# A linear attention and mixture-of-experts kernel: one weight transfer per expert, seven gather buffers, and more of the down projection in split form

## The reference

```python
x = _layernorm(x + attention(x))      # decayed linear attention, 16 heads
x = _layernorm(x + moe(x))

# moe, T = 4096 rows, H = 512, E = 64 experts, K = 6, CAP = 128, I = 192
scores = softmax(xf @ gate_w.T)
topk_w, topk_idx = top_k(scores, K)
gx = xp[buf_tok]                                      # (E, CAP, H) rows of each expert
gu = einsum('ech,ehi->eci', gx, gate_up_proj)         # 512 -> 384
g, u = split(gu, 2, axis=-1)
hid = silu(g) * u                                     # 192 wide
eo = einsum('eci,eih->ech', hid, down_proj) * buf_w   # 192 -> 512
routed = zeros.at[buf_tok].add(eo)
shared = silu(xf @ shared_gate_w.T) * (xf @ shared_up_w.T) @ shared_down_w.T
```

## Time and profile before

| | us |
|---|---|
| median of 3 runs | 913.0 |
| lowest, highest | 909.56, 913.59 |
| profiled execution, its own time | 914.21 |
| span of the profiled execution | 911.6 |
| PE busy | 892.3 |
| DVE busy | 718.9 |
| ACT busy | 549.0 |
| POOL busy | 488.1 |

### The profile page before, as it was taken

One profiled execution on the slowest core, in us unless ns is written; L12 is line 12 of the kernel. 1 busy time (PEld: TensorE's weight loads), 2 busy tenths in 40 slices (PEclk: granted clock), 3 DMA queues, 4 the chain that ended last, 5 costly groups with the idle time before them and its releaser, 6 DMA issues. The chain is left out here.

```text
span 911.6 us, 15597 instructions
## 1 busy us (share of the span) xinstructions
PE 892.3 (98%) x4635; PEld 727.5 (80%) x4635; DVE 718.9 (79%) x1422; ACT 549.0 (60%) x1208; POOL 488.1 (54%) x540
## 2 busy tenths in 40 slices
PE   8999999999999999999999999999999999999997
PEld 7788888888888788777888788888788888877875
DVE  6997887979788897898857788887778887736776
ACT  5532535434353443544558878888778888736785
POOL 2002366565566656577434656766566666533665
PEclk9999999999999999999999999999999999999999
DMA  6343563536263333439567999999999999959963
GB/s 211 97 161 116 145 140 103 133 89 173 74 188 96 123 103 116 144 101 336 181 224 238 333 360 354 357 337 323 348 342 347 336 346 324 298 106 391 378 249 129
DMA packets 111634, 203.95 MB, mean 224 GB/s; under 512 B 18496, under 2 KB 50240, under 8 KB 110528
## 3 DMA queue, kind: packets, MB, share of 16 engines
q1 hardware_dynamic: 91024, 159.87, 51.2%
q0 software_dynamic: 19520, 35.75, 16.3%
q10 hardware_dynamic: 1008, 7.34, 2.1%
HBM read 143.03 MB, written 59.88 MB: 223 GB/s over the span
## 5 line engine op out<-in xcount | busy, mean ns | idle before, releaser
L1612 POOL DMA_INDIRECT slot_table<-tokens,slot_of x162 | 180.3, 1113 | 86.9 <-issue 50.4
L1657 POOL DMA_INDIRECT acc_rows<-eo,table_sb x64 | 137.1, 2142 | 119.8 <-DMA acc_rows<-eo,table_sb 61.8
L1717 PE MATMUL bank<-x_hi,wqkv_hi 128*128 128x512 f32 x384 | 152.1, 396 | 1.6 <-DVE wqkv_lo L1022 1.6
L1717 PE MATMUL bank<-x_hi,wqkv_lo 128*128 128x512 f32 x384 | 150.1, 391 | 0.0
L1717 PE MATMUL bank<-x_lo,wqkv_hi 128*128 128x512 f32 x384 | 150.1, 391 | 0.0
L1454 DVE TENSOR_TENSOR wgu_lo<-wgu,wgu_hi 128x1536 fp32r<-128x1536 f32 x64 | 112.1, 1752 | 2.6 <-ACT wgu_hi L904 1.9
L904 ACT CAST wgu_hi<-wgu 128x1536 fp32r<-128x1536 f32 x64 | 94.2, 1473 | 1.6 <-issue 0.4
L1646 POOL DMA_INDIRECT xg<-x_rows,table_sb x64 | 73.4, 1147 | 36.3 <-issue 19.0
L1717 PE MATMUL bank<-wgu_hi,xgt_hi 128*128 128x384 f32 x256 | 91.9, 359 | 0.0
L674 ACT ACTIVATE e<-bank 128x512 f32<-128x512 f32 x64 | 38.0, 594 | 81.4 <-PE bank L1717 81.4
L1717 PEld LDWEIGHTS bank<-x_hi,wqkv_hi 128*128 128x128 f32 x384 | 72.2, 188 | 17.5 <-DVE wqkv_lo L1022 1.8
(11 more groups left out here) (198 smaller groups left out, 2300.0 us busy)
## 6 DMA issues: line engine op xcount, KB each, us to landing
wgu<-w_gu SPq DMA_DIRECT2D x64, 768.0 KB, 7.3
wdn<-w_down SPq DMA_DIRECT2D x64, 384.0 KB, 8.0
xres<-x SPq DMA_DIRECT2D x32, 256.0 KB, 3.4
x_turned<-x1t SPq DMA_DIRECT2D x32, 256.0 KB, 2.9
x_rows<-x SPq DMA_DIRECT2D x32, 256.0 KB, 3.1
acc_rows<-x SPq DMA_DIRECT2D x32, 256.0 KB, 2.8
fin<-acc_rows SPq DMA_DIRECT2D x8, 1024.0 KB, 11.9
odd<-acc_rows SPq DMA_DIRECT2D x8, 1024.0 KB, 13.9
```

The costliest lines, as they stand in the source:

```text
L1612: pool.indirect_dma_start(table_dram, bass.IndirectOffsetOnAxis(slot_of[:, i, k:k + 1], 0), tokens[:, i:i + 1], None, bounds_check=SLOTS - ...
L1657: pool.indirect_dma_start(acc_dram[e % 2], bass.IndirectOffsetOnAxis(table_sb[:, e:e + 1], 0), eo[eo_slot[e]][:, :], None, bounds_check=T ...
L1717: mm = pe.matmul(out_ap, a, b, start=first and i == 0, stop=final and i == len(products) - 1)
```

## The change

Three things are changed.

**Weights.** The gate, up and down weights of an expert stand side by side in DRAM (`w_expert`, 2304 floats per partition) and are loaded by one transfer (`load_expert`, 1152 KB) into one of five joint buffers. It waits for `eo_mm` of the expert five back, as the down weights did. Before the loop, expert 1 is loaded as a whole where its down weights were loaded.

**Gathers.** There are seven buffers instead of six, `gather` runs five experts ahead instead of four, and in a pass it stands before `add_rows`.

**Plain down rows.** For 40 of the 64 experts (`split_first(e)`: a unit in pass `e` or in pass `e-1`, so 0, 1, 3, 4, 6, 7, ...) the plain down rows are split too: ACT makes one more copy (`wdn_hi`, 128x512), DVE one more subtraction (`wdn_lo`, 128x512), ACT copies the turned hidden values in one instruction of 256 columns instead of two of 128, DVE's `het_lo` has 256 columns instead of 128, and PE runs three `fp32r` products instead of one in `f32`.

```diff
-    NG, ND, NXG, AHEAD = 5, 5, 6, 4
+    NW, NXG, AHEAD = 5, 7, 5
...
+    def split_first(e):
+        return any(fills_of[max(e - 1, 0):e + 1])
...
-            def load_gate_up(e):
-                if e >= NG:
-                    sp.wait_ge(gu_mm, e - NG + 1)
-                sp.dma_start(wgu_buf[e % NG][:, :, :], w_gu[e]).then_inc(gu_in[e % NG], 16)
-
-            def load_down(e):
-                if e >= ND:
-                    sp.wait_ge(eo_mm, e - ND + 1)
-                sp.dma_start(wdn_buf[e % ND][:, :], w_down[e]).then_inc(dn_in[e % ND], 16)
+            def load_expert(e):
+                if e >= NW:
+                    sp.wait_ge(eo_mm, e - NW + 1)
+                sp.dma_start(we_buf[e % NW][:, :], w_expert[e]).then_inc(we_in[e % NW], 16)
...
             sp.wait_ge(state_done, STEPS)
-            for e in range(2, NG - 1):
-                load_gate_up(e)
-            load_down(2)
+            load_expert(2)
...
             sp.wait_ge(heads_mm, NB)
-            load_down(3)
+            load_expert(3)
             sp.wait_ge(shared_split, 2)
-            for e in range(2):
-                load_gate_up(e)
+            load_expert(0)
...
             sp.wait_ge(shared_split, 2 + SC)
-            for e in range(2):
-                load_down(e)
+            load_expert(1)
...
-            load_gate_up(NG - 1)
-            load_down(ND - 1)
-            for e in range(NE):
-                if e + NG < NE:
-                    load_gate_up(e + NG)
-                if e and e - 1 + ND < NE:
-                    load_down(e - 1 + ND)
+            for e in range(4, NE):
+                load_expert(e)
...
             def split_down_of(e):
-                act.wait_ge(dn_in[e % ND], 16 * (e // ND + 1))
+                act.wait_ge(we_in[e % NW], 16 * (e // NW + 1))
                 if e >= 2:
                     act.wait_ge(eo_mm, e - 1)
-                w, mix = wdn_buf[e % ND], wdn_mix[e % 2]
+                w, mix = wdn_buf[e % NW], wdn_mix[e % 2]
+                if split_first(e):
+                    act.copy(wdn_hi[e % 2][:, :], w[:, 0:D])
...
-                act.copy(hid_et[e % 2][:, :], ht_ps[:, 0:P])
-                act.copy(het_hi[e % 2][:, :], ht_ps[:, P:2 * P]).then_inc(het_hi_done, 1)
+                if split_first(e):
+                    act.copy(het_hi[e % 2][:, :], ht_ps[:, 0:2 * P]).then_inc(het_hi_done, 1)
+                else:
+                    act.copy(hid_et[e % 2][:, :], ht_ps[:, 0:P])
+                    act.copy(het_hi[e % 2][:, P:2 * P], ht_ps[:, P:2 * P]).then_inc(het_hi_done, 1)
...
+                if split_first(e):
+                    dve.tensor_tensor(wdn_lo[e % NW][:, :], w[:, 0:D], wdn_hi[e % 2][:, :].bitcast(F32), ALU.subtract)
...
+                cols = slice(0 if split_first(e) else P, 2 * P)
+                dve.tensor_tensor(het_lo[e % 2][:, cols], ht_ps[:, cols], het_hi[e % 2][:, cols].bitcast(F32),
...
             for e in range(NE):
+                if e + AHEAD < NE:
+                    gather(e + AHEAD)
                 if e >= 2:
                     add_rows(e - 2)
-                if e + AHEAD < NE:
-                    gather(e + AHEAD)
...
-                chain(eo_ps[:, :], [(hid_et[e % 2][:, :], wdn_buf[e % ND][:, 0:D])], first=False).then_inc(eo_mm, 1)
+                if split_first(e):
+                    products = three(het_hi[e % 2][:, 0:P], het_lo[e % 2][:, 0:P], wdn_hi[e % 2][:, :], wdn_lo[e % NW][:, :])
+                else:
+                    products = [(hid_et[e % 2][:, :], wdn_buf[e % NW][:, 0:D])]
+                chain(eo_ps[:, :], products, first=False).then_inc(eo_mm, 1)
```

More of the change, by code:

```diff
@@ L89, in build @@
                                                           for s in ("sum", "mean", "square", "rstd", "shift")]
-    wgu_at = [both.at + 4 * i * KC * GU for i in range(2)]
-    wgu_buf = [both.place(f"wgu{i}", [P, KC, GU]) for i in range(2)]
-    wdn_buf = [both.place(f"wdn{i}", [P, DN]) for i in range(2)]
+    we_at = [both.at + 4 * i * WE for i in range(2)]
+    we_buf = [both.place(f"we{i}", [P, WE]) for i in range(2)]
     att = Map(nc, both.at, end)
@@ L197, in build @@
     late = Map(nc, projected_end, kept_from)
-    wgu_at += [late.at + 4 * i * KC * GU for i in range(NG - 3)]
-    wgu_buf += [late.place(f"wgu{i}", [P, KC, GU]) for i in range(2, NG - 1)]
-    wdn_buf += [late.place(f"wdn{i}", [P, DN]) for i in range(2, ND - 1)]
+    we_at += [late.at + 4 * i * WE for i in range(2)]
+    we_buf += [late.place(f"we{i}", [P, WE]) for i in range(2, 4)]
     assert late.at >= projected_end + 8 * 4 * BT
@@ L224, in build @@
     eo.append(late.place("eo3", [P, D]))
[L225 to L228, removed]
+    we_at += [late.at + 4 * i * WE for i in range(NW - 4)]
+    we_buf += [late.place(f"we{i}", [P, WE]) for i in range(4, NW)]
+    wdn_hi = [late.place(f"wdn_hi{i}", [P, D], F32R) for i in range(2)]
+    het_hi = [late.place(f"het_hi{i}", [P, 2 * P], F32R) for i in range(2)]
+    het_lo = [late.place(f"het_lo{i}", [P, 2 * P], F32R) for i in range(2)]
+    wdn_lo = [Map(nc, at + 4 * KC * GU, at + 4 * (KC * GU + D)).place(f"wdn_lo{i}", [P, D], F32R) for i, at in enumerate(we_at)]
+    wgu_buf = [we[:, 0:KC * GU].rearrange("p (k n) -> p k n", k=KC) for we in we_buf]
+    wdn_buf = [we[:, KC * GU:WE] for we in we_buf]
+    wgu_lo = [Map(nc, at, at + 4 * KC * GU).place(f"wgu_lo{i}", [P, KS, GU], F32R) for i, at in enumerate(we_at)]
     fin_map = Map(nc, both.at - 2 * 4 * (KC * GU + DN), both.at)
@@ L1453, in split_expert @@
                 dve.wait_ge(wgu_hi_done, e + 1)
[L1454 removed]
+                dve.tensor_tensor(wgu_lo[e % NW][:, :, :], wgu_buf[e % NW][:, 0:KS, :], wgu_hi[e % 2][:, :, :].bitcast(F32),
                                   ALU.subtract).then_inc(wgu_lo_done, 1)
@@ L1963, in down @@
                     pe.wait_ge(eo_done, e)
-                products = [(part[e % 2][:, :], wdn_mix[e % 2][:, :]) for part in (het_hi, het_lo)]
+                products = [(part[e % 2][:, P:2 * P], wdn_mix[e % 2][:, :]) for part in (het_hi, het_lo)]
                 chain(eo_ps[:, :], products, final=False)
-                chain(eo_ps[:, :], [(hid_et[e % 2][:, :], wdn_buf[e % ND][:, 0:D])], first=False).then_inc(eo_mm, 1)
+                if split_first(e):
[3 more added lines that the diff above has]
+                chain(eo_ps[:, :], products, first=False).then_inc(eo_mm, 1)
             for _ in range(BEFORE_EXPERTS[0]):
@@ L1986, in _ @@
                 for k in range(KS):
-                    products += three(xgt_hi[e % 2][:, k, :], xgt_lo[e % 2][:, k, :], wgu_hi[e % 2][:, k, :], wgu_lo[e % NG][:, k, :])
+                    products += three(xgt_hi[e % 2][:, k, :], xgt_lo[e % 2][:, k, :], wgu_hi[e % 2][:, k, :], wgu_lo[e % NW][:, k, :])
                 chain(gu_ps[e % 2][:, 0:GU], products).then_inc(gu_mm, 1)
@@ L2026 @@
         "decay_param": decay, "gate_t": a["L0_ffn_gate_w"].T,
-        "w_gu": gu, "w_down": down,
+        "w_expert": np.concatenate([gu.reshape(experts, P, -1), down], axis=2),
         "sg_t": a["L0_ffn_shared_gate_w"].T, "su_t": a["L0_ffn_shared_up_w"].T, "sd_t": a["L0_ffn_shared_down_w"].T,
```

19 lines of the change are left out of this document (8 added, 11 removed).

## The result

The changed kernel takes 929.6 us (median of 4 runs, 923.8 to 933.9) against 913.05 for the kernel before. The ratio of the runs is 1.0179, with a 95% interval of 1.0151 to 1.0207. The forecast was 913.4, range 905 to 921, so the change is slower where I expected no difference, and outside the range.

A forecast was written before the change was run, and what follows sets the result against it. PE bounds the kernel, an ACT and DVE chain setting the turning in second passes. 914.2 + 2.4 - 4.2 + 2.2 = 914.6 for the profiled execution, 1.2 above the median, so 913.4 us, range 905 to 921.

The forecast's parts named there:

- Part 1: Splitting plain down rows: PE's saving becomes waiting, a longer ACT and DVE chain costs; +2.4 us, bounds -6.8 and +10.
- both mechanisms that I described: Second passes: ACT and DVE chain 0.09 us longer; 8 first passes: PE waits for late het_lo, 0.08 us counted.
- Part 2: Gathers issued earlier: removes 2.5 us of waits and 1.7 of slow clock; -4.2 us, bounds 0 and -4.2.
- The 1.7 us of slow clock: Share of the gathers' gain: slow clock removed together with the 2.5 us of waits; 1.7 us of 4.2.
- the jam: Pass 32: POOL waits 1.94 us for an addition, the gather behind it comes late, PE stands 2.04 us.
- Part 3: Joint weight transfer asked for later: lateness behind three x1t_stage loads, 0.7 us each; +2.2 us, bounds 0 and 6.6.
- so I put it at 6.5 to 8 us: Joint transfer's landing time after issue, 6.5 to 8 us, against a shortest lead of 7.35: just in time.
- The bytes are the same.: Joint weight transfer: same bytes, only how early gate and up weights are asked for changes; no other price.
- The result buffers are four deep, so I count that at 0.: POOL's additions are issued some 1.1 us later; with four result buffers this costs 0 us.
- B: Weights late at ACT's wgu_hi in every triple's unit pass, from a landing of 8.3 us; 931 or 921 us; chance 0.22.
- A: PE's work counts: the split gives its full 6.8 us and the gathers theirs; 902.0 us; chance 0.18.
- C: Only the gathers matter, the split and the joint weights cost nothing; 908.8 us; chance 0.12.

The follow-up runs named there:

- two_loads: Changed kernel, but gate/up and down weights in two transfers again, the first released by the gate and up products as before; 912.7 us.
- gathers_only: Changed kernel with two weight transfers as before and no split, so only the gathers are changed; 909.9 us.
- no_split: Changed kernel with no expert's plain down rows split (all products in f32), joint late transfer kept; 926.0 us.
- late_two: gathers_only, but the gate and up load waits as the down load does, both issued in a row; 914.2 us.
- late_one_wait: late_two, but ACT's rounding of the gate and up weights waits for both transfers of its expert; 927.4 us.
- six_joint: Kernel before with joint transfers, six joint buffers, asked for a pass earlier than with five; rows of 9216 bytes, no split; 936.9 us.
- six_small: six_joint, but weights laid out in DRAM so that the transfer moves rows of 3072 bytes; 912.9 us.
- depth_only: gathers_only, but with the addition ahead of the gather; seven buffers and five ahead kept; 909.9 us.
- add_first: Changed kernel, but in each pass the addition is issued ahead of the gather, as before; 927.6 us.
- small_rows: no_split, but weights laid out in DRAM so that the one late transfer moves rows of 3072 bytes; 929.5 us.
- row_halves: no_split, but two transfers of 64 partitions each, rows of 9216 bytes, ACT waiting for both; 1045.1 us.
- col_thirds: no_split, but three transfers by columns of 768 floats per partition, ACT waiting for all three; 927.1 us.
- six_mid: six_joint, but weights laid out in DRAM so that the transfer moves rows of 4608 bytes; 918.1 us.
- less_weights: no_split, but from expert 5 on the transfer brings only 1728 of 2304 floats per partition; 910.4 us.

## Why the prediction was wrong

**Part 1 was right.** Foretold +2.4 us, measured +2.8 (two_loads against gathers_only, 912.7 and 909.9; 3.0 between their profiled loops). Pass by pass the two profiles show both mechanisms that I described. In 12 of the 20 triples the first pass mostly gets shorter by the 0.17 us of the split, the second longer by 0.24, and the triple loses 0.08 on average; I had 0.09 for the longer chain. In the other 8 (I had counted 8) the down products of the first pass wait for the late `het_lo`: that pass is 0.2 us longer or more, twice 0.6, the second gives back about 0.1, and the triple loses 0.22. I had 0.17.

**Part 2 was right in kind, one third too large.** Foretold -4.2 us, measured -2.9 (912.7 to 909.9, same runs). For the profiled execution the 4.2 was right: its loop took 332.0 us and that of gathers_only 328.0, and passes 34 and 35 alone make 3.5 of the difference. The 1.7 us of slow clock in the 4.2 are half of 3.4 us: the trace of the kernel before has the clock at 0.50 of full speed from 656.73 to 660.14 us, just behind PE's wait of 2.04 us, and with that the 10 us of the earlier trace rows come to 0.83. But I took that execution's stall and slow clock for typical. It was 1.2 us above the median, and I took these off as well, so a part of the jam was counted twice.

**Part 3 was wrong, and it is nearly the whole error.** Foretold +2.2 us, bounds 0 and 6.6. Measured +16.1 without the split, +16.9 with it, and +26.3 on the kernel before. Three steps were wrong or fell short.

1. *"so I put it at 6.5 to 8 us"*. The landing was 8.9 us, above the 8.3 from which ACT waits. The lead, from the issue to the moment when ACT wants the weights, was right: I read 7.35 at the shortest and about 10 elsewhere, and in no_split it is 7.1 at the shortest and 9.9 in the median. So it is the landing that was mis-sized, and with it the price: I charged lateness behind the three `x1t_stage` loads alone, while ACT's `wgu_hi` waits 10 times in the changed kernel, 9 of them in unit passes. The joint semaphore holds the gate and up weights back until the down weights' bytes are in. With two arrivals they land after 7.9 us, inside the 8.3, and the late request costs 4.3 us (late_two), within my bounds; with ACT waiting for the down weights as well, after 9.6 us, it costs 13.2 more (late_one_wait).
2. *"The bytes are the same."* The rows are not. With rows of 9216 bytes in place of 3072 other queues' transfers land later, and that is worth 24 us between six_joint and six_small. The sum had no price for them. The runs show the effect on both sides: with short rows additions land after 9.3 us in place of 9.8 and gathers after 7.7 in place of 8.4, and the weights after 10.1 in place of 8.5 (medians of six_small and of six_joint). By what mechanism they do not show.
3. *"The result buffers are four deep, so I count that at 0."* The additions went out later by 2.7 us, not 1.1 (in gathers_only at the least 3.5 us behind their `eo`, before 0.8), and while they land in time this does cost nothing: gathers_only and depth_only take the same 909.9. What the step missed is that additions to one sum wait for each other. Before, they took 9.1 us to land, the next one started 0.85 us later, and two passes take 10.3; there was 0.4 us of room for each. When landing takes 9.9 us, the chain of additions is slower than the passes, the lag grows until the four buffers are used up, and they only delay the stall. In the changed kernel an addition is asked for 3.6 us behind its `eo` for expert 0, 8.4 for expert 10, and 8 to 15 us from expert 14 to expert 49; in that stretch `eo` of the expert four later often starts 0.08 us after the landing. This is where the lateness of additions comes out, and not a third cause: in add_first `eo` never waits, PE waits for gathered rows instead, and the time is 927.6.

Some waits also cost more than their length, since a slow clock followed them: in the changed kernel PE's waits of 2.27 us at 663.3 and of 2.23 us at 724.1 were each followed by 3.4 us at 0.50 of full speed, though its longest, 3.40 us at 705.6, was not. I had such a term in part 2 and none in part 3.

In the joint kernels one of the two causes is enough for most of the loss, and the other one is partly hidden behind it. Without long rows but late with one arrival: 929.5 (small_rows). With long rows and early: 936.9 (six_joint, with shallow gathers). Only with both gone is the time back: 912.9 (six_small). So the two prices do not add up to the loss, and undoing one of them alone would have looked like proof of its innocence.

**The range.** The bounds of the parts do not add up as I wrote them. 913.0 with +10, 0 and +6.6 is 929.6, not 928. The measured 929.6 meets that bound by accident, since 10 of it stood for the split, which cost 2.8. For 8 in 10 I had then cut the upper end to 921.

**The rivals.** B, slower by weights late at `wgu_hi`, named one of the two places, the point of decision (8.3 us, measured 8.9) and nearly the time (931 and 921). It had 0.22. The time is partly luck: `wgu_hi` waits for 10.3 us in all and in 9 of 20 unit passes, not in each, and 18.3 us of ACT's waiting is for additions, which B did not have. A was ruled out for the reason given: the split costs 2.8 us instead of saving 6.8. C's number, 908.8, is what gathers_only took, to 1.1 us.

gathers_only and depth_only (909.9 us each) beat the kernel before by 0.1% to 0.5% and the changed kernel by 2%. The part of the change worth keeping is the seventh buffer and the fifth expert ahead. No run has the changed kernel's split or its deeper gathers together with short rows and an early joint request, so whether a joint load can be kept beside them at no cost is open.

## What to carry to other kernels

When two loads are joined, list their arrivals, not only their issues: the reader of the first part now waits for the second part's bytes (13.2 us in late_one_wait). Look at a load's row length too where the DMA engines have hardly any room left (a busy share of 0.98 in six_joint, 1.01 in six_small): from six_joint to six_small, rows of 3072 bytes in place of 9216 brought additions 0.5 us and gathers 0.7 us earlier and the load itself 1.6 us later. And a stream that waits for its own last transfer (additions to one sum) has to be compared with the pass in microseconds per item, since buffers do not help it. Where a waiting engine's work moves off PE, find the chain that starts ahead of the saved work; if the next wait hangs on that chain, the saving is a longer wait.

## What the runs showed of the hardware

Transfers to 64 of the 128 partitions were slow. In row_halves a packet of 9216 bytes took 582 ns on average (median 598), where it took 382 in no_split (median 347). The DMA answer for 480 to 800 us of row_halves:

```profile
DMA packets 16391, 76.07 MB, mean 238 GB/s; under 512 B 2731, under 2 KB 2731, under 8 KB 10654
...
we<-w_expert SPq DMA_DIRECT2D x88, 576.0 KB, 11.6
...
xg<-x_rows,table_sb POOLq DMA_INDIRECT x42, 15.3
```

The loop moved 238 GB/s in place of 325, and gathers, whose own packets also took 291 ns in place of 196, landed after 15.3 us. Splitting the load by partitions was not neutral (1045 us against 926); splitting it by columns nearly was (col_thirds, 927.1). Why the weights' packets take 1.5 times as long to 64 partitions no run here shows.

The highest rates of the changed kernel's page stand behind its loop: 391 and 385 GB/s in the two slices from 836 to 883 us, where the 14 slices from 488 to 813 us have 280 to 363.

DMA packets of one size mostly take much the same time: over 480 to 800 us of the kernel before, 98% of the packets of additions and of gathers, 95% of those of 6144 bytes and 62% of those of 3072 lie within 10% of their median. The medians over 480 to 800 us are 121 ns for 3072 bytes and 234 for 6144 (kernel before), 178 for 4608 (gathers of the kernel before, weights of six_mid) and 347 for 9216 (no_split), that is 25 to 27 bytes per ns for each engine; an addition's 2048 bytes take 176 ns, 11.6 bytes per ns. By these, as an estimate, one expert takes an engine 8 x (234 + 121) ns for weights, 8 x 176 for additions and 4 x 178 for gathers, 4.96 us, against an average pass of 5.17 us in the kernel before and 5.11 in gathers_only. The loop was within 3 to 4% of the DMA engines' pace as well as close to PE's. The busy rows of the page say this only as a "9". The engine table for 480 to 800 us has a DMA share of 1.01 for the kernel before and 0.94 for less_weights.
